# Second cross attention: rows normalised one phase earlier, and ten of a group's sixteen gathers at its beginning

## The reference, cut to what matters

```python
x = x + sum over k < 8 of weight[token, k] * y[slot[token, k]]      # end of layer 0
xn = layernorm(x)                                                   # mean 0, variance 1 over 256
q, k, v = xn @ Wq, ctx @ Wk, ctx @ Wv                               # 16 heads of 128
q, k = rmsnorm(q) * gq, rmsnorm(k) * gk
p = softmax(q @ k.T / sqrt(128))                                    # 257 keys
x = x + (p @ v) @ Wo
```

## Time and profile before

| | us |
|---|---|
| median of 3 timed runs | 2556.38 (2551.67 to 2558.78) |
| the profiled execution | 2556.95 |
| its span, first to last instruction | 2554.9 |
| PE busy in the span | 2466.8 (97%) |
| DVE, ACT, POOL busy | 1304.8, 1310.7, 753.5 |
| second cross attention, in the span | about 1258 to 1870 |

### The profile page before, as it was taken

The page is one execution under the profiler, slowest core; times in us unless marked ns, Lnnn a source line. Parts: engine busy times, 40 slices in busy tenths (PEclk is TensorE's granted clock), DMA queues, the critical chain, the costliest instruction groups (busy, mean ns, idle before and its releaser), DMA issues. The chain is left out here.

```text
span 2554.9 us, 61096 instructions
## 1 busy us (share of the span) xinstructions
PE 2466.8 (97%) x19044; PEld 1873.8 (73%) x19044; DVE 1304.8 (51%) x4749; ACT 1310.7 (51%) x4901; POOL 753.5 (29%) x897
## 2 busy tenths in 40 slices
PE   8999999999999999999889999999989999999988
PEld 6888888877644444544567887788878888888877
DVE  4555555556577764444455444555434444444434
ACT  3555555554366666666576556666623333333342
POOL 1222222337546540001443333331151111111032
PEclk9999999999899999999999999999999999999999
DMA  6222222110140004441454444442372000000033
GB/s 208 65 66 66 66 66 66 57 56 1 47 165 13 1 18 120 125 122 42 102 158 118 114 117 111 125 124 88 88 178 89 8 8 8 8 8 7 10 96 122
DMA packets 176868, 195.20 MB, mean 76 GB/s; under 512 B 40074, under 2 KB 142536, under 8 KB 175971
## 3 DMA queue, kind: packets, MB, share of 16 engines
q1 hardware_dynamic: 153074, 157.81, 21.2%
q0 software_dynamic: 17744, 32.60, 5.6%
q10 hardware_dynamic: 5920, 3.28, 0.7%
HBM read 150.44 MB, written 56.62 MB: 81 GB/s over the span
## 5 line engine op out<-in xcount | busy, mean ns | idle before, releaser
L299 PE MATMUL rt_kn_key_ps<-moe_w_wk,all_big 128*128 128x512 f32 x560 | 250.2, 600 | 0.8 <-DVE moe_kn_stats L348 0.4
L858 ACT ACTIVATE xa_probsT<-xa_probsT_ps 128x256 f32<-128x256 f32 x512 | 190.8, 374 | 97.6 <-PE xa_probsT_ps L692 90.7
L2449 PEld LDWEIGHTS sa_work_ps<-sa_xnT,all_big 128*128 128x128 f32 x2048 | 230.0, 192 | 9.6 <-issue 6.2
L2449 PE MATMUL sa_work_ps<-sa_xnT,all_big 128*128 128x128 f32 x2048 | 233.5, 276 | 2.8 <-POOL all_big L2304 2.3
L715 PE MATMUL xa_misc_ps<-cross_folded,xa_mixT 128*128 128x256 f32 x1024 | 230.1, 380 | 0.0
L715 PEld LDWEIGHTS xa_misc_ps<-cross_folded,xa_mixT 128*128 128x128 f32 x1024 | 194.1, 190 | 28.9 <-issue 2.9
L692 PE MATMUL xa_probsT_ps<-all_ident,xa_probs 128*128 128x128 f32 x1024 | 197.4, 275 | 7.4 <-DVE xa_probs L999 6.7
L999 DVE TENSOR_SCALAR xa_probs<-xa_probs,xa_share 128x257 f32<-128x257 f32 x512 | 187.3, 387 | 14.3 <-DVE xa_share L997 0.5
L299 PEld LDWEIGHTS rt_kn_key_ps<-moe_w_wk,all_big 128*128 128x128 f32 x560 | 104.8, 192 | 120.6 <-issue 114.5
L850 ACT ACTIVATE xa_probs<-xa_probs,xa_shift,xa_row_scale 128x257 f32<-128x257 f32 x256 | 152.6, 596 | 78.7 <-DVE xa_shift L983 78.4
L320 ACT ACTIVATE rt_kn_key_ps<-rt_kn_key_ps 128x128 f32<-128x128 f32 x560 | 148.4, 265 | 85.0 <-PE rt_kn_key_ps L299 85.0
(11 more groups left out here) (402 smaller groups left out, 5022.5 us busy)
## 6 DMA issues: line engine op xcount, KB each, us to landing
all_big<-rk SPq DMA_DIRECT2D x256, 128.5 KB
xa_pair<-pairs SPq DMA_DIRECT2D x64, 256.5 KB, 14.5
pairs<-all_big SPq DMA_DIRECT2D x64, 128.5 KB, 3.1
moe_w_wk<-in_ctx_dram SPq DMA_DIRECT2D x64, 128.0 KB, 2.5
pairs<-xa_keys SPq DMA_DIRECT2D x64, 128.0 KB, 2.1
cross_folded<-in_L_ffn_w_gate_dram SPq DMA_DIRECT2D x32, 192.0 KB, 2.6
cross_folded<-in_L_ffn_w_up_dram SPq DMA_DIRECT2D x32, 192.0 KB, 2.8
ff_rows<-pairs SPq DMA_DIRECT2D x35, 128.0 KB, 2.1
```

Of the source, the lines that this page charges most:

```text
L299: pe.matmul(self.key_ps[m % self.banks][0:n, :], self.ctxT[:, c * P:c * P + n], self.wk[:, q * 512:(q + 1) * 512], start=True, stop=True). ...
L858: act.activation(probsT[:, b % 2, :, r * P:(r + 1) * P], probsT_ps[s % 2][:, 0:KB * P].rearrange("p (k n) -> p k n", k=KB), ACT.Copy).then ...
L2449: ins = pe.matmul(ps[:, j, :], w[:, c, h * HD:(h + 1) * HD], xnT[:, c, :], start=(c == 0), stop=(c == NC - 1))
```

## The change

The statistics of group i+2 move into the query phase of pass i, between the third and the fourth `flip_sums`, right behind the last take, and its normalising behind the first two weighed rows of group i+1. POOL's `norm_scale` moves behind the four row scales. The last pass keeps the old places. The first ten gathers of a group are issued in one run at the first item; the other six come two at a time at items 1 to 3, behind the same waits as before.

```diff
+        FRONT = NB // 2 + 1
...
-            def keep_queries(g, more=False):
+            def keep_queries(g, link, more=False):
                 if layer == 1:
                     for r in range(R):
                         flip_sums(g, r)
...
+                        if more and r == R - 2:
+                            all_taken(g)
+                            row_stats(g + 1, link)
...
-                    if not last:
+                    if layer == 0 and not last:
                         if s == ROW_STATS:
-                            if layer == 1:
-                                all_taken(i)
-                            else:
-                                dve.wait_ge(x_loaded, 16)
+                            dve.wait_ge(x_loaded, 16)
                             row_stats(i + 1, link)
                         if s == ROW_STATS + R:
                             normalize(i + 1)
-                    elif layer == 1:
+                    elif layer == 1 and last:
...
-                    keep_queries(i + 1, more)
+                    keep_queries(i + 1, link, more)
                     for s in range(0, AHEAD, ROWS_AT_ONCE):
                         weigh_rows(i + 1, s)
+                        if more and s == 0:
+                            normalize(i + 2)
...
-                    if b == ROW_STATS // R + 1 and (layer == 1 or not last):
+                    if b == ROW_STATS // R + 1 and (last if layer == 1 else not last):
                         norm_scale(i + 1, link)
                     if more and b == 0:
                         next_places(i + 2)
-                    if more:
-                        if b:
-                            pool.wait_ge(mixed, i * NB + (RING + b))
-                            apart(pool, pool_passed)
-                        gather(range(b * PORTION, (b + 1) * PORTION))
+                    if more and b == 0:
+                        gather(range(FRONT * PORTION))
+                    elif more and b <= NB - FRONT:
+                        pool.wait_ge(mixed, i * NB + (RING + b))
+                        apart(pool, pool_passed)
+                        gather(range((FRONT + b - 1) * PORTION, (FRONT + b) * PORTION))
                 if layer == 1 and not last:
                     if more:
                         pool.wait_ge(gathered, i * (16 * G * K0) + 16 * K0 * (1 + G))
                     row_scales(i + 1, link)
+                    if more:
+                        norm_scale(i + 2, link)
```

More of the change, by code:

```diff
@@ L916, in _ @@
         def _(dve):
-            FIRST = 1 + EXP_AHEAD // ROWS_AT_ONCE
+            FIRST = 1 + EXP_AHEAD // ROWS_AT_ONCE + layer
             LINKS = 1 + ST // ROWS_AT_ONCE
@@ L1029, in iteration @@
             def iteration(i, last, more):
-                link = Chain(dve, dve_chain, i * LINKS + FIRST, passed)
+                link = Chain(dve, dve_chain, i * LINKS + FIRST - (1 if layer == 1 and last else 0), passed)
                 for s in range(ST):
@@ L1053, in iteration @@
                 if not last:
-                    keep_queries(i + 1, more)
+                    keep_queries(i + 1, link, more)
                     for s in range(0, AHEAD, ROWS_AT_ONCE):
                         weigh_rows(i + 1, s)
+                        if more and s == 0:
+                            normalize(i + 2)
                     for s in range(0, EXP_AHEAD, ROWS_AT_ONCE):
                         share_out(i + 1, s, link)
-                    assert link.n == LINKS, link.n
+                    assert link.n == LINKS - (1 if layer == 1 and not more else 0), link.n
                 for t in range(G):
@@ L1074, in _ @@
                 dve.tensor_scalar(any_diag[:, :], ident[0:B, 0:B], any_row[:, 0:1], None, ALU.mult).then_inc(any_ready, 1)
-            keep_queries(0, layer == 1)
+            keep_queries(0, link, layer == 1)
             if layer == 0:
@@ L1090, in _ @@
                 weigh_rows(0, s)
+                if layer == 1 and s == 0:
+                    normalize(1)
             for s in range(0, EXP_AHEAD, ROWS_AT_ONCE):
@@ L1102, in _ @@
             LINKS = 1 + NB if layer == 0 else 1 + R
-            FIRST = 1 if layer == 0 else 1 + R
+            FIRST = 1 if layer == 0 else 1 + R + 1
             def norm_scale(g, link):
@@ L1140, in iteration @@
             def iteration(i, last, more):
-                link = Chain(pool, pool_chain, i * LINKS + FIRST, pool_passed)
+                link = Chain(pool, pool_chain, i * LINKS + FIRST - (1 if layer == 1 and last else 0), pool_passed)
                 for b in range(NB):
@@ L1160, in iteration @@
                     row_scales(i + 1, link)
-                assert last or link.n == LINKS, link.n
+                    if more:
+                        norm_scale(i + 2, link)
+                assert last or link.n == LINKS - (1 if layer == 1 and not more else 0), link.n
             def next_places(g):
@@ L1198, in _ @@
                 row_scales(0, link)
+                norm_scale(1, link)
             assert link.n == FIRST, link.n
```

## The result

The changed kernel takes 2585.32 us (median of 4 runs, 2581.83 to 2589.42) against 2556.47 us, a ratio of 1.0116 (95% 1.0094 to 1.0138). The change makes it slower, by 28.9 us; the forecast was no difference. The profiled execution took 2589.42 us with a span of 2587.7 us, 32.8 us over before's span.

A forecast was written before the change was run, and what follows sets the result against it. PE was taken as busy nearly throughout, idling 11.05 us for late key scales on SP's queue over few DMA engines. Terms +2.1 - 1.0 - 0.2 = +0.9 us gave 2557.9, as a median 2557.3; range 2550.5 to 2564.5.

The forecast's parts named there:

- exchange of waits: Whole kernel: waits lost in pass 0 and won in later passes nearly cancel, -1.6 to +4 us; chance 0.60.
- rival (b): Row phases: the gather burst pushes the key scales' queue back every pass, up to +14.5 us, 2570.9; chance 0.10.
- price g: Delay one gather causes to key scales queued beside it: 0.35 us taken, between 0.13 and 0.71 us.
- step 1: Pass 0: the burst meets a full queue, six more gathers ahead of the last item's scales, +2.1 us.
- Step 2: Passes 1 to 5, last item: fewer gathers late against more at the beginning, -0.2 us a pass, -1.0 us in all.
- Step 3: Row phases: the statistics' stumble goes; waited downstream in passes 0 to 5, worth -0.2 us in pass 6.
- Steps 4 to 6: Query phases: moved statistics and normalising are covered by existing waits, and gathers land long before use; zero.
- Rival (a): Passes 1 to 5: the last item's five waits vanish, -8.35 us, 2548.0; chance 0.07 in full, 0.20 in part.

The follow-up runs named there:

- after_again: The changed kernel itself, unchanged, run again beside the kernel before: ratio 1.0093 (1.0072 to 1.0115).
- before_spread8: The kernel before with the repeat of each key scale load put outermost, so eight DMA engines serve it instead of four: 0.9972 of the kernel before.
- norm_spread8: The changed kernel with gathers put back to two at each item and key scale loads over eight engines instead of four: 0.9952 of the kernel before.
- norm_only: The changed kernel with its gathers put back, two at each item, keeping the moved normalising: 0.9999 of the kernel before.
- spread16_again: Repeat of the changed kernel with gathers put back to two at each item and key scale loads over sixteen engines: 0.9938 of the kernel before, 2586.81 us.

## Why the prediction was wrong

The forecast was an exchange of waits at 2557.3 us with 0.60. The time is its rival (b), the run pushes the key scales' queue back in every pass, which had 0.10 and 2570.9 us at its highest price; even that was 14 us short.

- **The price g, ahead of step 1, is the step that failed.** I took 0.35 us for every gather, read where two stand at an item, and 0.71 us as the upper bound. For couples 0.35 us is right: item 7's scales landed at 1702.31 in pass 5 and at 1775.05 in pass 6, 24.40 and 21.65 us after the first group of the earlier trace rows, 0.34 us more for each of eight gathers. (My reading from below, 0.13 us, took the use at 1776.98 for the landing.) But the change makes a run, and in a run a gather costs the key scales about 1.0 us: item 4's landed 16.9 us after their issue in place of 8.5, with eight gathers more. The bound was no bound: 0.71 us is what a gather cost the engines while little else moved. Its 4096 B packets took 0.35 us in the mean there, two for an engine. They took 0.41 us over passes 0 to 5 of before, 0.55 us of after, and 0.62 us in the first 16 us of after's passes 1 to 5. By rival (b)'s own sum, 31 g - 7.5, g = 1.0 gives +23.5 us; measured were 28.9 us, and 23.9 in after_again. The rule cited with (b), the Trainium skill (DMA: Bandwidth & Descriptors, "SWDGE vs HWDGE vs iDMA") on turns between queues, fits: item 4's loads, issued 4 us after the run had begun, were slowed at once.
- **Step 1 (pass 0, +2.1 us):** +11.5. With g = 1.0 it is +6. All sixteen gathers were out at 1313.86 + 1.00, but their last packets ended at 1323.6. By the landing of item 5's scales sixteen gathers had been issued in place of six, and it came 13.9 us later in the pass, 1.4 us each.
- **Step 2 (passes 1 to 5, -0.2 us each):** +3.3 to +4.7. The gathers fewer at the end were real, worth 2.3 us at items 6 and 7, and so was the pause ahead of item 5's scales, worth 2.2 us, more than the 1.5 I had given it. Against them stood not 2.45 but 8.4 us at item 4.
- **The granted clock, which no step had,** is not what was missing. It falls behind the waits of passes 0 to 4, but nothing of it is left in the length of a pass, as the result shows.
- **Step 3 (pass 6, -0.2 us):** -1.15, the right sign and too small. The idle time before one transpose isn't all that statistics and normalising cost among DVE's rows; where no key scale is waited for this is worth 0.5 to 1.0 us in each of passes 1 to 5 as well (before_spread8 74.5 to 74.9, norm_spread8 73.7 to 74.1).
- **Steps 4 to 6 (the query phase, 0):** right, shown by norm_only.
- **Rival (a), the waits go:** the run makes none of them go. They go with more engines for the loads, for which the prediction had the rule: that with sixteen a gather would delay nothing held where two stand at an item (spread16_again), and not for the run of ten on kind S.

## What to carry to other kernels

Before moving transfers about beside a queue that runs on few DMA engines, take that queue's own landings, with the transfers and without them, in the arrangement that is planned: a price read from couples was three times too low for a run. Count what else stands between two landings, and compare with a stretch that has none of the transfers, as pass 6 here. Then find the one landing that ends the stage; what is late before it, a wait or a slower clock, costs nothing by itself. Last, look whether the queue can be given more engines: a repeat over eight in place of four was worth 0.28% by itself, and one over sixteen 0.67% together with the moved normalising, while no other placement of the gathers gained anything. Keep runs of software gathers short, two at a time in this kernel, and judge by more than one chip: on one kind the run still cost 21.5 us when no key scale was waited for.

## What the runs showed that I had not expected

- A gather's packets grow dearer with the number of gathers in flight: a 4096 B packet took 0.16 us at best, 0.41 us in the mean of before's pairs and 0.62 us in the mean of the runs of ten, while the key scales' own 4112 B packets stayed at 0.18 us in the mean in both.
- On three chips, and not in the traces of kind Q, PE's semaphore increments came 1.5 to 7 us late behind six or more gathers in a row, in a bunch, as the gathers drained; with 64 rows a gather the delay was as long.
- Reading one copy 32 times with sixteen engines is no slower than reading four copies with four: in passes 1, 2 and 6 the loads of items 4 and 5 landed 2.6 to 3.3 us after the last issue in place of 5.6 to 7.5, and the last of the four was issued 1.3 to 1.6 us after the first instead of 2.1 to 2.6 us.
